# Vision transformer layer with experts: the Newton steps of three norms on GpSimd

## What is computed

```python
x = layernorm(patches @ patch_w + patch_b, ln_g, ln_b) + positions       # norm 0
x1 = window_attention(ff(x)) + x
h = concat(cls, ff(x1) + x1)
h = h + sparse_attention(layernorm(h))           # norm 2; 12 heads, the 26 best of 65 keys are kept
h = h + shared(layernorm(h)) + routed(layernorm(h))   # norm 3; the best 6 of 128 experts
# layernorm(x) = (x - mean) / sqrt(var + 1e-5)
```

## Time and profile before

| what | value |
| --- | --- |
| median of 3 runs | 936.86 us (936.58 to 936.96) |
| the profiled execution | 934.52 us, span 932.7 us |
| mean granted TensorE clock | 0.970 |
| busy: PE, DVE | 830.9 us (89%), 722.6 us (77%) |
| busy: ACT, POOL | 345.7 us (37%), 307.7 us (33%) |
| chain that ended last | DVE 48%, PE 38%, issue 5%, ACT 4% |

### The profile page before, as it was taken

How to read it: one execution, slowest core, us unless ns; L and a number is a source line. 1 busy time by engine, 2 the same in 40 slices (tenths; PEclk the granted TensorE clock), 3 DMA queues, 4 the chain that set the end, 5 groups by cost and what they waited for, 6 DMA issues and landing times.

```text
span 932.7 us, 22271 instructions
## 1 busy us (share of the span) xinstructions
PE 830.9 (89%) x7603; PEld 731.8 (78%) x7603; DVE 722.6 (77%) x3781; ACT 345.7 (37%) x971; POOL 307.7 (33%) x354
## 2 busy tenths in 40 slices
PE   1687899899899899899899999999999999999993
PEld 1576688788788788888789989998879767676762
DVE  3356899999899899999999979799675465656562
ACT  0335554544544544545445344432210122222220
POOL 7021213403313223224123131121121276766664
PEclk8699999999999999999999999999998899999997
DMA  7410000101101101001001100010112466666651
GB/s 222 117 52 1 2 27 23 40 17 37 30 17 36 30 11 39 17 24 34 26 23 44 31 6 21 22 45 20 45 28 64 112 160 144 160 144 160 144 129 24
DMA packets 48231, 54.25 MB, mean 58 GB/s; under 512 B 9013, under 2 KB 41531, under 8 KB 48108
## 3 DMA queue, kind: packets, MB, share of 16 engines
q1 hardware_dynamic: 39180, 43.89, 16.4%
q0 software_dynamic: 6352, 7.62, 5.6%
q10 hardware_dynamic: 2608, 1.60, 0.7%
HBM read 42.40 MB, written 10.69 MB: 57 GB/s over the span
## 4 chain that ended last, share of the span: by engine, by line
DVE 48%; PE 38%; issue 5%; ACT 4%; SPq 2%; DVEq 1%; POOL 0%; DMA 0%; ACTq 0%; POOLq 0%
DVE b_arena L1500 9%; PE p_big L999 3%; PE p_shared L831 3%; DVE b_top_a L1486 3%; PE p_big L686 3%; PE p_shared L832 3%; PE p_big L687 2%; DVE b_top_d L1486 2%; PE p_shared L837 2%; DVE b_arena L1548 2%; DVE b_top_b L1486 2%; DVE b_top_c L1486 2%; PE p_small L693 2%; DVE b_rstd L1238 2%; PE p_big L1004 2%
## 5 line engine op out<-in xcount | busy, mean ns | idle before, releaser
L1769 POOL DMA_INDIRECT b_arena<-x_rows,b_index x44 | 68.0, 1544 | 49.4 <-DVE b_index L1565 36.6
L686 PE MATMUL p_big<-b_xT,b_ff1a 128*128 128x128 f32 x384 | 77.5, 285 | 1.4 <-ACT b_xT L1029 1.4
L1703 POOL TENSOR_TENSOR b_arena<-b_kY,b_mask_k 64x256 f32<-64x256 f32 x16 | 9.7, 608 | 205.9 <-ACT b_kY L1054 205.9
L687 PE MATMUL p_big<-b_xT,b_ff1b 128*128 128x128 f32 x384 | 76.5, 282 | 0.0
L1029 ACT COPY b_xT<-p_small 128x256 f32<-128x256 f32 (+1 forms) x97 | 35.4, 377 | 83.4 <-PE p_small L677 83.3
L1734 POOL TENSOR_TENSOR b_arena<-b_arena 128x768 f32<-128x768 f32 x16 | 27.0, 1687 | 117.8 <-DVE b_arena L1512 117.8
L686 PEld LDWEIGHTS p_big<-b_xT,b_ff1a 128*128 128x128 f32 x384 | 61.6, 200 | 2.5 <-ACT b_xT L1029 2.5
L999 PE MATMUL p_big<-b_xeT,b_arena 128*116 128x192 f32 x320 | 61.9, 336 | 0.0
L687 PEld LDWEIGHTS p_big<-b_xT,b_ff1b 128*128 128x128 f32 x384 | 60.7, 199 | 0.0
L720 PE MATMUL p_big<-b_arena,b_q_blk 128*128 128x256 f32 (+3 forms) x256 | 48.9, 334 | 12.5 <-ACT b_q_blk L1061 12.4
L720 PEld LDWEIGHTS p_big<-b_arena,b_q_blk 128*128 128x128 f32 x256 | 41.3, 190 | 19.4 <-POOL b_arena L1703 12.6
(11 more groups left out here) (379 smaller groups left out, 2548.1 us busy)
## 6 DMA issues: line engine op xcount, KB each, us to landing
b_arena<-in_w_gate_up SPq DMA_DIRECT2D x20, 464.0 KB
b_arena<-in_w_down SPq DMA_DIRECT2D x20, 336.0 KB
b_xp<-in_xp SPq DMA_DIRECT2D x16, 384.0 KB, 3.1
b_arena<-in_w_gate_up SPq DMA_DIRECT2D x40, 116.0 KB
xT_rows<-b_xmT SPq DMA_DIRECT2D x16, 128.0 KB, 1.8
b_xT_late<-xT_rows SPq DMA_DIRECT2D x16, 128.0 KB, 2.2
h_rows<-b_h SPq DMA_DIRECT2D x16, 96.0 KB, 1.6
x_rows<-b_xm SPq DMA_DIRECT2D x32, 48.0 KB, 2.0
```

The source lines that it names most:

```text
L686: mm(o, ff1a[:, c * 128:(c + 1) * 128], xTa[s][:], start=True, stop=False)
L687: last = mm(o, ff1b[:, c * 128:(c + 1) * 128], xTb[s][:], start=False, stop=True)
L1769: G.indirect_dma_start(xg[s][0:rows, h, :], None, x_rows[:, :], bass.IndirectOffsetOnAxis(index[s][0:rows, h:h + 1], 0)).then_inc(S(f"gath ...
```

## The change

A new generator `variance` takes the place of `statistics` and `layernorm` in the three norms of each tile (index s: 3 for norm 0, 1 for norm 2, 2 for norm 3). It stops after the start value and the scaled variances. The six Newton instructions are made by a new GpSimd generator, `inverse_deviation`, as TENSOR_SCALAR instructions of one column with two operands of one column each, and a column that holds 3.0 is new. GpSimd takes the steps up on the semaphores `n0_var`, `n2_var`, `n3_var` and gives back `n0_rstd`, `n2_rstd`, `n3_rstd`; for norms 2 and 3 VectorE waits for the latter before its last step. The class tokens' norms stay as they were.

```diff
+            def variance(src, s, rows, name):
...
+                ts(rstd[s][:].bitcast(i32), var[s][:].bitcast(i32), -0.5, float(0x5f3759df - (3 << 23)), op0=ALU.mult, op1=ALU.add)
+                tt(scaled[s][:], var[s][:].to_broadcast([128, 3]), scales[:], ALU.mult).then_inc(S(f"{name}_var"), 1)
...
+                if s == 2:
+                    yield from variance(x[:], s, 128, "n3")
+                    yield "norm3"
+                    dve.wait_ge(S("n3_rstd"), v)
+                    ts(xm[s][:], x[:], mv[s][:, 0:1], rstd[s][:], op0=ALU.subtract, op1=ALU.mult).then_inc(S("xm_ready"), 1)
+                    return
...
+            V.memset(three[:], 3.0)
...
-                yield from statistics(patch_x[:], 3, 128, "n0", S("n0_rstd"))
+                yield from variance(patch_x[:], 3, 128, "n0")
...
-                for last in layernorm(norm2[:], h2[v % 2][:], 1, v, 128, "n2"):
...
+                yield from variance(h2[v % 2][:], 1, 128, "n2")
+                yield "norm2"
+                dve.wait_ge(S("n2_rstd"), v)
+                ts(norm2[:], h2[v % 2][:], mv[1][:, 0:1], rstd[1][:], op0=ALU.subtract, op1=ALU.mult).then_inc(S("n2_ready"), 1)
...
+            def inverse_deviation(s, v, n):
+
+                yield f"newt{n}"
+                pool.wait_ge(S(f"n{n}_var"), v)
+                r, q = rstd[s][:], newton[s][:]
+                for k in range(3):
+                    if k:
+                        pool.wait_ge(pool_step, noted("newton1", s))
+                    gts(q, r, r, scaled[s][:, k:k + 1], op0=ALU.mult, op1=ALU.mult).then_inc(pool_step, note("newton0", s))
+                    yield
+                    pool.wait_ge(pool_step, noted("newton0", s))
+                    last = gts(r, three[:], q, r, op0=ALU.add, op1=ALU.mult)
+                    if k < 2:
+                        last.then_inc(pool_step, note("newton1", s))
+                        yield
+                last.then_inc(S(f"n{n}_rstd"), 1)
```

The table of orders is new for all five engines. Two of its lines, from GpSimd's words:

```diff
-        keys_queries3 top_keys2 patches5*2 positions5 top_keys3 routes1*5 tokens4 tokens5 top_keys3
+        keys_queries2 top_keys1 top_keys2 tokens3 routers1*6 tokens4 keys_queries3*6 top_keys2 keys_queries3
```

More of the change, by code:

```diff
@@ L284 @@
+        keys_queries16 shared11 weigh15*2 shared11 shared12*2 weigh15 shared12*2 weigh15*2 shared12 shared13*2
+        routers15 weigh16*2 routers15 shared13*2 weigh16 shared13 shared14*2 weigh16*2 shared14*2 class_tile16
+        routers16 shared14 routers16 shared15 class_tile16 shared15 class_tile16 shared15*2 ranks16 shared15
+        shared16*2 ranks16 shared16*2 ranks16*2 shared16 shared17 ranks16 shared17 ranks16 shared17*2 ranks16
+        shared17
     """,
@@ L433, in tower_kernel @@
         var, newton, scaled = each("var", [128, 1]), each("newton", [128, 1]), each("scaled", [128, 3])
-        scales = sb("scales", [128, 3])
+        scales, three = sb("scales", [128, 3]), sb("three", [128, 1])
         xT = {0: sb("xT0", [128, 256]), 1: sb("xT1", [128, 256 + 64])}
@@ L1244, in inverse_deviation @@
                 dve.wait_ge(step, noted("newton1", s))
+            def variance(src, s, rows, name):
+                V.bn_stats(stat[s][0:rows, :], src).then_inc(step, note(name + "_stat", s))
+                yield
+                hold(dve, step, noted(name + "_stat", s))
+                V.bn_aggr(mv[s][0:rows, :], stat[s][0:rows, :]).then_inc(step, note("aggr", s))
+                yield
+                dve.wait_ge(step, noted("aggr", s))
+                ts(var[s][:], mv[s][:, 1:2], 1e-5, None, op0=ALU.add).then_inc(step, note("eps", s))
+                yield
+                dve.wait_ge(step, noted("eps", s))
+                ts(rstd[s][:].bitcast(i32), var[s][:].bitcast(i32), -0.5, float(0x5f3759df - (3 << 23)), op0=ALU.mult, op1=ALU.add)
+                tt(scaled[s][:], var[s][:].to_broadcast([128, 3]), scales[:], ALU.mult).then_inc(S(f"{name}_var"), 1)
             def statistics(src, s, rows, name, done=None):
@@ L1714, in keys_queries @@
             def keys_queries(v):
+                yield from inverse_deviation(1, v, 2)
                 yield from four_keys(1, v, kT2[0:64, 1, :, :], NKEY)
@@ L1789, in _ @@
             pool.wait_ge(loads_tokenizer, 16 * len(tokenizer_loads))
-            interleave("pool", *every(patches, positions, tokens, keys_queries, top_keys, routes), (TILES, route(1, 1, B, TILES)),
+            interleave("pool", *every(patches, positions, tokens, keys_queries, top_keys, routers, routes), (TILES, route(1, 1, B, TILES)),
                        (NT, gathers()))
```

421 lines of the change are left out of this document (196 added, 225 removed).

## The result

The kernel with the change takes 969.63 us, median of 6 runs (965.14 to 970.38), against 936.91 for the kernel before: a ratio of 1.0343, 95% interval 1.0319 to 1.0367. It is 33 us slower where I forecast 15 us faster. The profiled execution has a span of 968.0 us (before 932.7).

The account below looks back on a forecast made before the run. VectorE was taken as the fuller of two nearly full engines, with TensorE. Per tile 2.5 - 0.2 - 1.1 + 0.2 = 1.4 us, over 11 tiles 15.4 off 936.86, giving 922 with the memset; range 911 to 940.

Parts of the forecast that it names:

- What bounds it: Middle part, 90 to 490 us: VectorE, busy 378.65 of 400 us, is the fuller engine; TensorE has 365.95.
- What leaves VectorE, 2.5: 18 Newton instructions a tile leave VectorE: 1.56 us for the second and third norms, 0.97 for the first, together 2.5.
- What stays although its row goes: VectorE held up by GpSimd's long product finds another victim; the hold averages 1.35 us a tile, before 1.15: -0.2.
- What is added: Six dependent GpSimd instructions a norm, 0.33 us start to start; VectorE waits 0.69 and 0.41 for two chains: -1.1 a tile.
- my upper bound: GpSimd step of 0.44 us start to start, giving a chain of 2.85 and VectorE waits of 1.36 and 1.08.
- the sum at nought: At a GpSimd step of 0.44 us the tile's sum was 2.5 - 0.2 - 2.5 + 0.2, no gain.
- The first norm's chain ... I cost it at nothing: First norm's chain on GpSimd ends some 0.7 us later, but the h0 that follows has spare time: cost nothing.
- What TensorE makes of it, +0.2: Late second norm stops TensorE, leaving most of VectorE's 0.85 us wait uncollected: +0.2 a tile, between 0 and 0.85.
- My own sign: Sign that the forecast is wrong: TensorE's share of the middle part, 90 to 490 us, doesn't rise from 0.91.
- Outside the middle part ... under 1 us: Outside 90 to 490 us, the constant's memset and the first tiles' bare chains cost under 1 us.
- the dear instruction: Slower rival: two-operand form costs 0.415 more per GpSimd instruction; at 0.6 a step 958 us, deciding from 0.45; 14%.
- The shared port: No-difference rival: VectorE and GpSimd obstruct each other; 0.47 us for each of three chains cancels the 1.4, 937 us; 7%.

Follow-up runs that it names:

- e10: Kernel before, its order word for word, with only norm 0's six Newton steps moved from VectorE to GpSimd: 935.50 us, ratio 0.9991.
- e12: e5 with two Newton steps in place of three in the tiles' norms, each GpSimd chain 0.88 us shorter: 921.72 us, ratio 0.9851.
- e14: e5 with the 3.0 in each step's second instruction as an immediate instead of a column operand: 937.08 us, ratio 1.0009.
- e15: Kernel before with two fitted Newton steps in place of three, still on VectorE in the old order: 928.93 us, ratio 0.9937.
- e5: Changed kernel with GpSimd's subtraction of the greatest scores queued ahead of b_norm, gain and positions in 9 tiles: 947.58 us, ratio 1.0108.
- e6: Changed kernel's order with all Newton steps back on VectorE, norm 0's six in one piece behind the start value: 951.23 us, ratio 1.0160.
- e4: Changed kernel with ScalarE's copy b_xT put ahead of the second attention's exponential again in 11 tiles: 947.22 us, ratio 1.0112.
- e9: Changed kernel with both mends: norms 2 and 3 back on VectorE as in e3, subtraction ahead as in e5: 936.82 us, ratio 0.9999.
- e13: e5 with the Newton steps of tiles 1 to 4 back on VectorE and nothing else changed: 946.03 us, ratio 1.0108.
- e3: Changed kernel with the Newton steps of norms 2 and 3 back on VectorE, norm 0's left on GpSimd: 954.31 us, ratio 1.0196.
- e11: Kernel before's order with all 18 Newton steps of a tile on GpSimd, the move without the new layout: 956.32 us, ratio 1.0214.

## Why the prediction was wrong

- **What bounds it**: half right. VectorE was the fuller engine, but e10 took six of its instructions a tile away for 0.2 us. What e12 and e14 show on the path is the chain of a norm together with what waits for it.
- **What leaves VectorE, 2.5**: as busy time it left; as time of the tile it was worth less. e15 drops six instructions a tile, and from tile 5 to tile 15 a tile takes 35.59 instead of 36.26: 0.11 for each, where I counted 0.13 and 0.16. I also misread: 0.195 is the share of each of four instructions up to a reciprocal that waits for none of them. The chained steps start 0.20 to 0.25 apart, as the rows between show (VectorE, before):

```profile
252.77 0.16 DVE L1238 SCALAR_TENSOR_TENSOR b_rstd<-b_newton,b_rstd 128x1 f32<-128x1 f32 x1
252.97 0.22 DVE L1235 SCALAR_TENSOR_TENSOR b_newton<-b_rstd,b_scaled 128x1 f32<-128x1 f32 x1
253.22 0.16 DVE L1238 SCALAR_TENSOR_TENSOR b_rstd<-b_newton,b_rstd 128x1 f32<-128x1 f32 x1
```

- **What stays although its row goes**: the hold by GpSimd's product found another victim, as I said: the router's first addition takes 1.83 us (at 254.57) in every other tile, some 1.6 too much, and in the tiles between the router's second addition takes 0.62 (at 294.87) where 0.28 is usual. That is 1.0 on average, not 1.35 and less than before's 1.15: the term should have been some +0.2, not -0.2.
- **What is added**: mis-sized, within my bounds. I took 0.33 from start to start, it is 0.44, my upper bound. For that bound I had waits of 1.36 and 1.08; measured 1.01 and 1.05. And I had the sum at nought there: in e5, where the stall is mended, a tile takes 36.41 against 36.26. The waits were computed rightly, with the wrong row for the step: the new form has two column operands, and the nearest row had to be sought among instructions with such operands. That the whole tile agrees too is in part luck, since the sum has no term for the new layout, and with every step on VectorE (e6) that layout takes 37.13 a tile. The measured record is 0.34, and the chain goes by 0.44. By the factor of the Trainium skill (GPSIMD Engine Reference, "Performance versus the Vector engine") the record was an estimated 0.41; the trace lies below that and above my 0.25. The Trainium skill (Perfetto Trace Analysis, "GPSIMD Engine Instruction") says to time GpSimd from start to start and not by the reported duration; by that rule, the trace agrees.
- **"The first norm's chain ... I cost it at nothing"**: this step failed. I named the cover, the other image's work on TensorE, and looked at what waits for h0. I did not look at what is queued behind the chain: on GpSimd the subtraction, on ScalarE the copy behind its exponential. It costs 22 us (e4, e5), in about equal parts waits and slower clock. The other 11 of the 33 us are gone when norms 2 and 3 go back as well (e9, 936.82).
- **What TensorE makes of it, +0.2**: TensorE waits for b_norm 12.3 us in ten tiles, before 5.6 in the same stretch: 0.7 a tile more, near my bound of 0.85. What I left out is the clock. My own sign came: TensorE's share of the middle part did not rise from 0.91, it fell to 0.90.
- **"Outside the middle part ... under 1 us"**: wrong. At tile 7 9.5 us are lost; by e13, which starts from e5, some 3.4 by the bare chains of the first tiles and 6 by the layout. Behind the addition of tile 16 another 4.0 are lost, in e5 too; with norms 2 and 3 on VectorE it is 1.2 to 2.4 (e3, e6, e9).
- **The rivals**: the dear instruction had the right sign and the wrong reason: it decides from 0.45, the step is 0.44. Its 0.415 for two operands was partly right in kind (e14: 0.07 for one). The shared port shows at most now and then (one step of 1.16 in e11, whose cause isn't shown; in the changed kernel's middle part no step is over 0.51), and VectorE's searches stayed at 0.21. What the Trainium skill (Perfetto Trace Analysis, "Optimizing Scalar/DVE Operations") warns of is not what cost the time here. That the new order itself could be worse I had no rival for, although all five tables were new.

Together: 9.5 us by tile 7, then 2.3 a tile to tile 15, 3.5 at tile 16 and 4.0 behind it, which makes the 35.3 of the span; the medians lie 33 apart. Of the 48 us between forecast and result 22 are the stall (e4, e5) and 15 the gain that my own sum loses at a step of 0.44; the other 11 fit what is lost in the filling and behind tile 16, though no run takes these apart.

## What to carry to other kernels

When a chain moves to another engine, follow the queue behind it, and then the queue of the engine that waits for that queue's next item; a result with room to spare can stand ahead of one that has none. Price a small instruction on GpSimd by its start-to-start time with the same kinds of operands, and count the chain as many times as it stands bare, the filling of the pipeline included. Swapping two words in a strict order tests such a stall in one run. Once it was mended and the chain shortened, the same move won 2.0% over the kernel before, 1.2% of it beyond what the shorter chain gives on VectorE.

## What the runs showed of the hardware

- A GpSimd TENSOR_SCALAR of one column takes 0.34 us and its dependent successor starts 0.44 after it; with one column operand instead of two, 0.27 and 0.37. VectorE's chained steps started 0.20 to 0.25 apart.
- After 4 us with TensorE mostly idle the granted clock stood at 0.50 for 6 us of full work, so that 1.0 us a tile of standing still cost 2.1.
